# Attention plus pair-product layer on one Trainium2 core: steps of 128 keys by 512 queries, and half of the exponents taken from kept maximum pieces

## The reference, cut to what matters

```
# layer 0: x = x + attention(groupnorm(x))
f = Wq @ xn + bq            # 32 x 4096
g = Wk @ xn + bk            # 32 x 4096
h = Wv @ xn + bv            # 256 x 4096
s[i, j] = sum_k f[k, i] * g[k, j]
beta = softmax(s, axis=i)   # for each j, over all 4096 i
o[c, j] = sum_i h[c, i] * beta[i, j];  x = x + gamma * o
# layer 1: x = x + pairs(groupnorm(x))
y = relu(bn(w1 @ xn + b1))  # 32 x 4096
packed = y[rows] * y[cols]  # all 528 pairs of the 32 channels
x = x + relu(bn(w2 @ packed + b2))
```

## Time and profile before

| | |
|---|---|
| median of 3 runs | 2221.08 us |
| the profiled execution, first to last instruction | 2216.6 us, 4.5 us less than the median; its time with what lies around the span is not given apart |
| TensorE matmul busy | 2164.2 us, 98% |
| VectorE busy | 1857.5 us, 84% |
| ScalarE busy | 1734.7 us, 78% |
| GpSimd busy | 801.5 us, 36% |
| mean granted TensorE clock | 0.998 |

### The profile page before, as it was taken

One profiled execution on the slowest core, in us unless ns is written; L12 is line 12 of the kernel. 1 busy time (PEld: TensorE's weight loads), 2 busy tenths in 40 slices (PEclk: granted clock), 3 DMA queues, 4 the chain that ended last, 5 costly groups with the idle time before them and its releaser, 6 DMA issues.

```text
span 2216.6 us, 43342 instructions
## 1 busy us (share of the span) xinstructions
PE 2164.2 (98%) x16662; PEld 1607.4 (73%) x16662; DVE 1857.5 (84%) x3220; ACT 1734.7 (78%) x2806; POOL 801.5 (36%) x832
## 2 busy tenths in 40 slices
PE   4899999999999999999999999999999999999999
PEld 3577777777777777777777777777787777777754
DVE  7788888878888888888888898888988888888677
ACT  5578888878777788888777788888877778777777
POOL 2111222223233443453533344444344333343346
PEclk9999999999999999999999999999999999999999
DMA  6001111111123333322233233333212222122212
GB/s 198 14 6 20 20 26 23 27 28 28 31 60 89 82 89 80 82 64 71 62 81 85 65 83 88 89 79 85 62 35 58 61 59 53 34 50 52 62 35 76
DMA packets 186957, 132.58 MB, mean 60 GB/s; under 512 B 135520, under 2 KB 142432, under 8 KB 186720
## 3 DMA queue, kind: packets, MB, share of 16 engines
q1 hardware_dynamic: 186752, 129.81, 23.7%
HBM read 71.83 MB, written 19.92 MB: 41 GB/s over the span
## 4 chain that ended last, share of the span: by engine, by line
PE 90%; DVE 5%; ACT 2%; issue 1%; DMA 1%; POOL 0%; SPq 0%; ACTq 0%; POOLq 0%; DVEq 0%
PE acc L1766 16%; PE acc L1758 16%; PE acc L1759 16%; PE tps L1546 9%; PE sps L1565 8%; PE tps L1616 3%; PE acc L1540 3%; PE acc L1729 2%; PE acc L1725 2%; PE acc L1726 2%; PE tps L1618 2%; DVE mx L801 2%; PE acc L1616 1%; PE tps L1580 1%; DVE pl L842 1%
## 5 line engine op out<-in xcount | busy, mean ns | idle before, releaser
L1300 ACT ACTIVATE ph<-sps,esc 128x512 f16<-128x512 f32 x904 | 619.9, 686 | 318.7 <-PE sps L1565 312.7
L1758 PE MATMUL acc<-hth,ph 128*128 128x257 f16 x3488 | 814.7, 274 | 1.0 <-ACT ot L1323 0.9
L1759 PE MATMUL acc<-htl,ph 128*128 128x256 f16 x3488 | 813.4, 273 | 0.0
L801 DVE TENSOR_REDUCE mx<-tps 128x1 f32<-128x512 f32 x904 | 617.9, 686 | 224.4 <-PE tps L1546 214.1
L842 DVE TENSOR_TENSOR pl<-p,ph 128x512 f16<-128x512 f32 x904 | 737.3, 818 | 65.5 <-ACT p L1303 63.1
L1303 ACT ACTIVATE p<-sps,esc 128x512 f32<-128x512 f32 x904 | 616.8, 682 | 0.0
L1766 PE MATMUL acc<-hth,pl 128*128 128x257 f16 x3488 | 527.9, 273 | 0.0
L1766 PEld LDWEIGHTS acc<-hth,pl 128*128 128x128 f16 x3488 | 340.5, 98 | 134.6 <-issue 0.3
L1759 PEld LDWEIGHTS acc<-htl,ph 128*128 128x128 f16 x3488 | 341.4, 98 | 117.2 <-issue 0.3
L1546 PE MATMUL tps<-fst,gst 96*128 96x512 f16 x1024 | 390.7, 383 | 16.1 <-DVE mx L801 11.0
L1758 PEld LDWEIGHTS acc<-hth,ph 128*128 128x128 f16 x3488 | 341.1, 98 | 57.4 <-ACT ot L1323 2.7
(11 more groups left out here) (258 smaller groups left out, 2553.5 us busy)
## 6 DMA issues: line engine op xcount, KB each, us to landing
rt<-turned SPq DMA_DIRECT2D x96, 256.0 KB, 4.6
xt<-x SPq DMA_DIRECT2D x36, 512.0 KB, 3.7
xb<-x SPq DMA_DIRECT2D x32, 512.0 KB, 4.9
out<-zt SPq DMA_DIRECT2D x45, 256.0 KB, 2.7
yb<-turned SPq DMA_DIRECT2D x36, 128.0 KB, 2.6
rt<-turned SPq DMA_DIRECT2D x72, 64.0 KB, 5.0
turned<-yb SPq DMA_DIRECT2D x12, 256.0 KB, 2.4
out<-fst SPq DMA_DIRECT2D x8, 256.0 KB, 2.0
```

The lines of the kernel that those rows point to most:

```text
L801: V.reduce_max(mx[:, tile, c:c + 1], tps[par][:], AX).then_inc(t_free[par], 1)
L1300: A(ph[:, v % SLOTS], sps[v % 2][:], ACT.Exp, scale=esc[:]).then_inc(ph_ok, 1)
L1758: mm(acc[j][:, 0:C + 1], w, hth[:, i], start=(t == 0), stop=False)
L1759: mm(acc[j][:, 0:C], w, htl[:, i], start=False, stop=False)
```

## The change

A step becomes one tile of 128 keys by 512 queries (eight steps to a tile, 128 tiles, again 1024 steps).

- The scores of a step are now four matmuls of 128 columns, each with its own weights, instead of one of 512. A step's 12 value matmuls all add to one bank, `acc[tile % 2]`; `acc[2]` takes the turned rows of maxima and `acc[3]` is a second bank for pieces.
- From the third tile on, four steps of every eight (1, 3, 5, 7) are kept ones: 504 of the 1024 instead of 120. 520 steps make their scores instead of 904.
- A kept piece goes to `ks` by a VectorE `tensor_scalar` that writes the copy and its maximum in one instruction; ScalarE's copy and VectorE's separate maximum go. Both exps of a kept piece stay with ScalarE (`HIGH_BY_ACT` names all four, so `kept_high` does nothing). The low half stays with GpSimd, the turning with the transposing DMA, now four for each tile.
- The second exp of a made step writes over the scores in PSUM instead of `p32`, and VectorE reads it there; the bank is freed by VectorE (`pl_ok`), no longer by ScalarE.
- Maxima, their split, rows and row copy are done for each tile of 128 keys, 128 times on one column instead of 32 times on four. The division by the softmax sum is done once per tile by ScalarE (`divide`); two of four were on VectorE.
- Pieces run 18 ahead instead of 40, and the prologue's order is new. The buffers `ph` and `pl` have 2 slots instead of 3.
- The order of GpSimd and of the sync queue is written out by step `t`.

```diff
-KEPT_FROM = 2
-KEPT = 1
-PLACES = (5,)
-KEPT_STEPS = (4,)
+CHUNK_AT = (6, 3, 0, 4, 1, 5, 2, 7)
+KEPT_STEPS = (1, 3, 5, 7)
+PIECES = tuple(CHUNK_AT[s] for s in range(8) if s not in KEPT_STEPS) + tuple(CHUNK_AT[s] for s in KEPT_STEPS)
+FIRST_TILE = 2
+HIGH_BY_ACT = (0, 1, 2, 3)
+AHEAD = 18
+KS_RING = 6
+KB_RING = 3
+KT_RING = 4
-SLOTS = 3
+SLOTS = 2
...
+        pbank = [tps[0], tps[1], acc[3]]
...
+        def scored_at(w):
+            return w - 2 if w < (FIRST_TILE + 1) * NCH else w - 3
+        def lowered_at(w):
+            return w - 1 if w <= FIRST_TILE * NCH else w - 2
...
             def turn(tile, r):
-                sp.wait_ge(kl_ok, count_of(tile, r) + 1)
-                G = tile // QT - 1
-                if G >= KEPT_FROM:
-                    sp.wait_ge(p_free, G * NT + tile % QT * NCH + KEPT_STEPS[r] + 1)
-                sp.dma_start_transpose(kt[:, tile % QT, r], kb[:, r].rearrange("p e n -> p (e n)")).then_inc(kt_in[r], 16)
+                m = count_of(tile, r)
+                sp.wait_ge(kl_ok, m + 1)
+                if m >= KT_RING:
+                    sp.wait_ge(p_free, kept_step(m - KT_RING) + 1)
+                sp.dma_start_transpose(kt[:, m % KT_RING],
+                                       kb[:, m % KB_RING].rearrange("p e n -> p (e n)")).then_inc(kt_in[m % KT_RING], 16)
...
             def step_piece(u):
+                    m = count_of(tile, r)
+                    full(par)
+                    if m >= KS_RING:
+                        dve.wait_ge(kl_ok, m - KS_RING + 1)
+                    V.tensor_scalar(ks[:, m % KS_RING], pbank[par][:], 1.0, None, ALU.mult, ALU.max,
+                                    accum_out=mx[:, tile % 4, PIECES[place]:PIECES[place] + 1]).then_inc(t_free[par], 1)
...
-                V.tensor_tensor(pl[:, v % SLOTS], p32[:, v % 2], ph[:, v % SLOTS],
+                V.tensor_tensor(pl[:, v % SLOTS], sps[v % 2][:], ph[:, v % SLOTS],
                                 ALU.subtract).then_inc(pl_ok, 1)
...
+                        if t % NCH in (2, 4, 5, 7) and is_kept_tile(tile):
+                            kept_low(tile, (2, 4, 5, 7).index(t % NCH))
+                        if t % NCH == 7 and tile + 1 < TILES:
+                            split_max(tile + 1)
+                        if t == 2 and b and n >= 2:
+                            residual(n - 2, 1)
...
+                        if t >= 27 and b:
+                            product(n, t - 27)
...
             def powers(u):
-                if v >= 2:
-                    act.wait_ge(pl_ok, v - 1)
-                A(p32[:, v % 2], sps[v % 2][:], ACT.Exp, scale=esc[:]).then_inc(p32_ok, 1)
-            def keep(tile, r):
-                A(ks[:, r], tps[0][:], ACT.Copy).then_inc(t_free[0], 1)
+                A(sps[v % 2][:], sps[v % 2][:], ACT.Exp, scale=esc[:]).then_inc(p32_ok, 1)
...
+                        if s8 in (3, 5, 7) and is_kept_tile(tile + 1):
+                            for r in {3: (0, 1), 5: (2,), 7: (3,)}[s8]:
+                                kept_powers(tile + 1, r)
+                        if s8 == 5:
+                            if t > 5 or J:
+                                divide(tile - 1)
+                            if tile + 1 < TILES:
+                                row_copy(tile + 1, acc[2])
...
             def scores(u):
-                    pe.wait_ge(p32_ok, v - 1)
-                mm(sps[v % 2][:], fst[:, G // NCH % 2, tile * P:(tile + 1) * P], gst[:, keys_at(G)], start=True,
-                   stop=True).then_inc(s_mm, 1)
+                    pe.wait_ge(pl_ok, v - 1)
+                if u % NCH == 0:
+                    pe.wait_ge(m_ok, tile + 1)
                 for q in range(QT):
+                    at = c * CH + q * P
+                    last = mm(sps[v % 2][:, q * P:(q + 1) * P], fst[:, tile // NT % 2, at:at + P],
+                              gst[:, key_tile(tile)], start=True, stop=True)
...
+                        for q in range(QT):
+                            mm(bank[:, 0:C + 1], high[:, q], hth[:, c * QT + q], start=(s8 == 0 and q == 0), stop=False)
+                            mm(bank[:, 0:C], high[:, q], htl[:, c * QT + q], start=False, stop=False)
+                        step_piece(u)
+                        for q in range(QT):
+                            last = mm(bank[:, 0:C + 1], low[:, q], hth[:, c * QT + q], start=False,
+                                      stop=(s8 == NCH - 1 and q == QT - 1))
+                        if s8 == 2 and tile + 1 < TILES:
+                            rows(tile + 1, acc[2])
```

More of the change, by code:

```diff
@@ L176, in build @@
         h_mm, h_hi, h_lo = sem("h_mm"), sem("h_hi"), sem("h_lo")
[L177 to L178 removed]
+        t_mm = [sem(f"t_mm{i}") for i in range(3)]
+        t_free = [sem(f"t_free{i}") for i in range(3)]
         nm_ok = sem("nm_ok")
@@ L353, in kept_before, with made, step_of @@
[L353 to L360, removed]
+            return u // NCH >= FIRST_TILE and u % NCH in KEPT_STEPS
+        MADE = [u for u in range(ALL) if not kept(u)]
+        MADE_AT = {u: v for v, u in enumerate(MADE)}
+        def made(u):
+            return MADE_AT[u]
+        def step_of(v):
+            return MADE[v]
@@ L371, in build, with casts_until, kept_step @@
-        MADE = [u for u in range(B * STEPS) if not kept(u)]
-        def step_of(v):
-            return MADE[v]
-        def tile_at(u, place):
-            tile = (u + AHEAD - place) // NCH
-            return tile if (u + AHEAD - place) % NCH == 0 and FIRST_TILE <= tile < TILES else None
-        def tile_before(u, place):
-            return tile_at(u - NCH, place)
+        def casts_until(m):
+            return sum(k % KEPT not in HIGH_BY_ACT for k in range(m + 1))
+        def kept_step(m):
+            return NCH * (FIRST_TILE + m // KEPT) + KEPT_STEPS[m % KEPT]
@@ new lines, in step_piece @@
+                    if r < 0 or not is_kept_tile(tile):
+                        piece_max(tile, PIECES[place], par)
+                        return
+                    m = count_of(tile, r)
[4 more added lines that the diff above has]
+                                    accum_out=mx[:, tile % 4, PIECES[place]:PIECES[place] + 1]).then_inc(t_free[par], 1)
@@ L1152, in _ @@
                 low(("first", 0, c))
-            split_max(0)
+            for tile in range(2):
+                split_max(tile)
             for b in range(B):
@@ L1708, in attend @@
                         u = G * NT + t
-                        if u + 2 < B * STEPS and not kept(u + 2):
-                            if t + 2 == NT:
-                                pe.wait_ge(m_ok, G + 2)
-                            scores(u + 2)
+                        tile, s8 = u // NCH, u % NCH
+                        bank, c = acc[tile % 2], CHUNK_AT[s8]
+                        if u in SCORED:
+                            scores(SCORED[u])
                         if b and J and n >= 2 and t == 0:
@@ L1768, in attend @@
-                        if not kept(u):
-                            last.then_inc(p_free, 1)
+                        if s8 == 0 and t == 0 and J == 0 and b:
+                            pe.wait_ge(h_lo, 2 * G + 12)
+                        elif s8 == 0 and tile >= 2:
+                            pe.wait_ge(ot_act, tile - 1)
+                        for q in range(QT):
+                            mm(bank[:, 0:C + 1], high[:, q], hth[:, c * QT + q], start=(s8 == 0 and q == 0), stop=False)
+                            mm(bank[:, 0:C], high[:, q], htl[:, c * QT + q], start=False, stop=False)
```

486 lines of the change are left out of this document (199 added, 287 removed), and 9 rows, old and new, of the table ORDER.

## The result

The changed kernel takes 2292.87 us (median of 4 runs, 2287.84 to 2303.62) against 2219.68 us for the kernel before on the same chip. The ratio is 1.0336, 95% interval 1.0309 to 1.0363. It was forecast at 2143 us, faster. It is slower.

What follows compares the result with a forecast made beforehand. TensorE's issued columns were taken to bound the kernel. 2216.6 - 83 (score matmuls) - 7 (prologue) + 12 (waits) = 2139 us of span, so 2143 us as the median of runs; range 2118 to 2205 us.

Steps and rivals of the forecast that it cites:

- Score matmuls and their width: TensorE's steps: 384 fewer score matmuls save 83 us; four of 128 columns cost the same 0.22 us as one wide.
- Rival C: TensorE's narrow score matmuls cost more: about 2200 us (chance 0.05), or 2257 us at the upper bound (0.03).
- the sum: Whole span: 2216.6 us less 83 and 7, plus 12 for waits, gives 2139 us.
- ScalarE and VectorE: Loads per stage: ScalarE 55 of 61.2 us, hidden; VectorE 7 us less to do, at no cost to the time.
- Rival B: ScalarE, 90% busy and strictly in order, or the chain through it sets the pace: about 2187 us, chance 0.16.
- its split: GpSimd's split of the maxima: 3.05 us each, one column costing as four; three more a stage, 9.2 us.
- The prologue: Before the steps: 18 pieces ahead instead of 40 take 12 us off; first exp near 74 us.
- the term of -7 us: Prologue 12 us shorter, less 5 us of pieces that come back in the steps; bounds 0 and -8 us.
- What the added waits cost: TensorE's waits, chiefly through GpSimd's crowded steps 27 to 31: +12 us in all, bounds 0 and 32.
- The text on the transposing DMA: Sync queue's transfers: exps come 11 us before TensorE's use; low half 1.2 and transfer 3 leave some 5 us.
- rival D: GpSimd's split stands behind products awaiting the rotation; brackets: late low halves hold up VectorE's kept pieces; 2244 us, chance 0.12.

Runs made afterwards that it cites:

- the variant at 2164.6 us: Changed kernel with four `kb` slots (five of `ks`), GpSimd's products moved into the next stage, rotation and spreads issued in parts: 2164.57 us, ratio 0.9756.
- the last experiment: Against the variant at 2164.6 us, two of a tile's four float16 high halves made by VectorE instead of ScalarE: 2159.91 us, ratio 0.9734.

## Why the prediction was wrong, point by point

**Score matmuls and their width: right.** The kernel after in a stretch without waits, a made step, the next score group and a kept step:

```profile
255.41 0.27 PE L1720 MATMUL acc<-hth,ph 128*128 128x257 f16 x1
...
256.95 0.39 PE L1545 MATMUL sps<-gst,fst 128*128 128x128 f16 x4
257.17 0.27 PE L1720 MATMUL acc<-hth,kt 128*128 128x257 f16 x1
...
258.72 0.27 PE L1720 MATMUL acc<-hth,ph 128*128 128x257 f16 x1
```

The 13 instructions take 1.54 us, four narrow score matmuls 0.22 us (55 ns each), the kept step 1.55 us, as the earlier trace rows said. Rival C falls. The Trainium skill (TensorE: Matmul & The Clock Gate, Back-to-back issue gap) has about 81 ns per matmul at 128 columns in a sustained stream with a weight load each. The measurement decides against it for this kernel, where four in a row stand between wider ones; a longer run of narrow ones was not measured. TensorE's busy time in the variant at 2164.6 us bears the sum out within 9 us: 2090 us against 2164 - 83 = 2081.

**ScalarE and VectorE: right for single instructions, too high in the sum.** `pl` was priced near 690 ns, the copy with maximum at 742 ns, the exp into PSUM between 570 and 680 ns:

```profile
L844 DVE TENSOR_TENSOR pl<-sps,ph 128x512 f16<-128x512 f32 x520 | 357.9, 688 | 431.1 <-ACT sps L1288 427.7
L811 DVE TENSOR_SCALAR_CACHE_REDUCE ks<-acc 128x512 f32<-128x512 f32 x252 | 172.9, 686 | 103.9 <-PE acc L1525 78.7
L1288 ACT ACTIVATE sps<-sps,esc 128x512 f32<-128x512 f32 x520 | 338.7, 651 | 0.0
L1280 ACT ACTIVATE gst<-acc 3x128 f16<-3x128 f32 x127 | 34.2, 269 | 4.3 <-PE acc L1554 1.3
```

A row copy takes 0.27 us where up to 0.59 was priced. From 600 to 1050 us of the variant at 2164.6 us ScalarE is busy for 84% and VectorE for 70%; the working gives 90% and about 79%. Rival B as a load falls with the last experiment. It named the right engine, though: TensorE did wait for ScalarE, because ScalarE was made to wait.

**GpSimd: its split was overpriced, and its order was the trouble.** A split on one column takes eight instructions at 0.27 us, 618.29 to 620.36 us, 2.1 us and not 3.05 as on four columns. GpSimd was busy for 66% of the time from 600 to 1050 us in the variant at 2164.6 us, not 81%; the split accounts for about half of that difference. With this load and the products elsewhere the waits were gone: the place of the products did the harm.

**The prologue: 3 us shorter instead of 12.** The first exp of the steps starts at 82.60 us, where before it was 85.87 and where I expected 74. With the 5 us of pieces that come back in the steps, the term of -7 us was about +2. TensorE's pieces now wait five times, 9.6 us in all, for the spread of projections by DMA, where before they waited twice, for 2.9 us. The two longest:

```profile
49.27 0.82 PE L1525 MATMUL tps<-fst,gst 96*128 96x512 f16 x2 [4.23 <-DMA gst<-qkl]
61.01 0.61 PE L1525 MATMUL tps<-fst,gst 96*128 96x512 f16 x2 [2.51 <-DMA gst<-qkl]
```

**The failed step is "What the added waits cost": +12 us, with bounds 0 and 32.** Without it the sum was 2127 us of span, so the changed kernel's 2302 us leave 175 us for it, of which some 9 belong to the prologue. Part of the 175 is direct: TensorE was idle for 163 us, where the sum left 52 - 7 = 45, so 118 us more. The rest, 58 us, is busy time over 2081. Of it 49 us are gone in the variant at 2164.6 us, which does the same columns in 2090 us; the granted clock is 0.998 there and 0.977 here. Two things were wrong in that step.

First, it looked at one reader of a transfer. The text on the transposing DMA counted from the exps to TensorE's use, 11 us, less 1.2 and 3, and found "some 5 us" to spare (these terms leave 6.8, and 5.4 after the two exps themselves). The landing has a second reader, ScalarE, which needs the slot of `kb` three pieces later, and the diff showed it: `KB_RING = 3` and `landed(m - KB_RING)`. A tile's exps come at steps 3, 3, 5 and 7, so three pieces on is eight, six or only four steps later. Four steps are 2 x (1.76 + 1.55) = 6.6 us; two exps, a low half and a landing (1.4, 1.2 and 3.1 us) leave 0.9 of them. That shortest case, a tile's fourth piece, has 88 of the 189 us of ScalarE's waits. The sync queue was named ("they stand behind the rotation") but the rotation's 6.6 us and the spread's 8.4 were not priced, and the 3.0 us to landing of the earlier trace rows came from a stretch of batch 0 without rotations. With four slots 75 us of the 175 go, without the burst 66.

Second, the wait for the rotation was priced by way of the split, at 3.6 us each for nine. The 4.7 us behind that is the mean of nine waits of which one took 24.5 us; the other eight have 2.2. TensorE never waited for a split in the steps. The loss came over the low halves, `ks` and VectorE's pieces, a link that stood only in rival D's brackets. D thus had the right cause, the products' place in GpSimd's queue, by the wrong main path. Its number was too high: taking the products away is worth 45 to 58 us, not 113. There are 11 such waits, and they don't come in each of the 24 stages.

The 2292.87 us lie above every rival's time, the highest being 2257, and for the larger part by a cause that no rival named. Of what stays after both are mended, 2162 - 2127 = 35 us, 27 are idle time over the 45 and 9 busy time over the 2081. In the prologue 7 of the 35 lie: its first exp comes at 81.17 us there, 4.7 us earlier than before in place of 12. The others were not taken apart.

## What to carry to other kernels

When a resource moves into a ring, list every reader of its release and hold the number of slots against the longest time that the release can take, queues included, not the median. A transfer's time is the wait for its issue on an in-order queue plus its landing behind what is ahead; take both from the stretch with the most traffic. Before believing a gain on a full engine, ask of each engine that runs in order which of its instructions can stall it, since it is late with everything behind that one; put a wait that must be kept behind what others need.

## What the runs showed of the hardware that was not expected

- The transposing transfer of 128 x 1024 float16 from SBUF to SBUF costs the DMA engines about twice a plain one: from 262 to 400 us the DMA share was 0.46 with 38 of them, and 0.23 with 39 plain copies; landing 3.1 against 2.3 us. The Trainium skill (Advanced Engine Details and Errata, X-Bar Transpose (TRN2)) says that such transfers are as fast as regular ones on trn2; for this shape the measurement says otherwise.
- The landing of one kind of transfer ranged from 3.0 to 7.6 us in one run: median 5.3 us for the 35 transfers with a rotation between the low half and their issue, 3.1 us for the 378 with nothing between.
- VectorE's copy with maximum in one instruction takes 686 ns, no more than the maximum alone (689 ns), and an accumulator read of 0.08 us. In both cases VectorE's next instruction on a piece or a `pl` can start 0.61 us after it (254.86 to 255.47 us with the copy, 258.47 to 259.08 without). So keeping a piece cost VectorE nothing that these rows show.
- `pl` fell from 818 ns to 688 ns when one of its inputs came from PSUM in place of SBUF, while GpSimd was busier than before.
